# A three-sublayer decoder kernel on one core: new orders at four places of an iteration, x2's halves in exchanged banks, and the third residual's sums on GpSimd

## The reference, cut to what matters

```
x = layernorm(x + attention(x))         # q, k, v, 16 heads of 32, causal softmax, output projection, with biases
x = layernorm(x + wkv(decay, first, k=x, v=ctx))   # a recurrence over the 256 tokens, each channel alone
x = layernorm(x + gated_attention(x))   # 16 heads of q; ONE shared k and v per token: those of the head
                                        # whose gate is highest (v times the softmax value of that gate); causal
```

## Time and profile before

| what | value |
|---|---|
| median of 3 runs | 1510.12 us |
| the profiled execution's own time | 1509.66 us |
| its span, first to last instruction | 1507.8 us |
| mean granted TensorE clock | 0.989 |
| PE, DVE, ACT, POOL busy | 1397.5, 1095.7, 650.5, 378.6 us |

### The profile page before, as it was taken

One profiled execution on the slowest core, in us unless ns is written; L12 is line 12 of the kernel. 1 busy time (PEld: TensorE's weight loads), 2 busy tenths in 40 slices (PEclk: granted clock), 3 DMA queues, 4 the chain that ended last, 5 costly groups with the idle time before them and its releaser, 6 DMA issues.

```text
span 1507.8 us, 26652 instructions
## 1 busy us (share of the span) xinstructions
PE 1397.5 (93%) x9908; PEld 1112.9 (74%) x9908; DVE 1095.7 (73%) x2258; ACT 650.5 (43%) x1459; POOL 378.6 (25%) x520
## 2 busy tenths in 40 slices
PE   7887899999999999999999999999999999998796
PEld 6676778777777877777777777777777777876563
DVE  4464777777777777777777778777787776779753
ACT  3453435345353534535354453525444352544223
POOL 1244312222131222213122221312232232222200
PEclk9999999999999999999999999999999999999997
DMA  6531323324142332314333241333313233330210
GB/s 184 154 92 36 92 78 82 96 56 103 35 104 81 83 95 54 103 37 99 85 82 96 52 101 41 92 92 82 96 40 98 56 92 92 82 82 18 55 44 29
DMA packets 63199, 119.50 MB, mean 79 GB/s; under 512 B 14304, under 2 KB 32736, under 8 KB 63072
## 3 DMA queue, kind: packets, MB, share of 16 engines
q1 hardware_dynamic: 60128, 112.03, 29.4%
q10 hardware_dynamic: 2944, 5.77, 1.1%
HBM read 32.81 MB, written 8.39 MB: 27 GB/s over the span
## 4 chain that ended last, share of the span: by engine, by line
PE 63%; DVE 19%; issue 3%; SPq 2%; ACT 2%; DMA 1%; POOL 0%; ACTq 0%; POOLq 0%; DVEq 0%
PE po L591 7%; PE pp L486 6%; PE pp L488 6%; PE pp L487 6%; DVE neg_max L1527 5%; PE pw L486 4%; PE pw L488 4%; PE pw L487 4%; PE sk L564 3%; PE sq L532 3%; PE sk L511 3%; PE po L595 3%; PE po L605 3%; PE sq L511 3%; PE sq L526 2%
## 5 line engine op out<-in xcount | busy, mean ns | idle before, releaser
L1527 DVE TENSOR_REDUCE neg_max<-sq 128x2 f32<-128x512 f32 (+1 forms) x384 | 252.7, 686 | 126.7 <-PE sq L511 125.1
L1161 ACT ACTIVATE prob<-sk 128x512 f32<-128x512 f32 x384 | 215.9, 597 | 250.7 <-PE sk L511 248.0
L486 PE MATMUL pp<-xt_hi,w_hi 128*128 128x256 f32 x616 | 189.1, 307 | 18.7 <-DVE w_lo L1514 7.6
L488 PE MATMUL pp<-xt_hi,w_lo 128*128 128x256 f32 x616 | 175.8, 285 | 0.0
L487 PE MATMUL pp<-xt_lo,w_hi 128*128 128x256 f32 x616 | 175.7, 285 | 0.0
L1172 ACT ACTIVATE o_ch<-po 128x512 f32<-128x512 f32 x128 | 76.2, 595 | 167.0 <-PE po L595 167.0
L486 PEld LDWEIGHTS pp<-xt_hi,w_hi 128*128 128x128 f32 x616 | 120.0, 195 | 23.2 <-issue 19.4
L2048 POOL TENSOR_TENSOR w_ev<-w_e,w_val 128x256 f32<-128x256 f32 x64 | 45.8, 716 | 360.0 <-ACT w_e L1218 319.3
L511 PE MATMUL sk<-mask_kq,ident_b 128*128 128x256 bf16 (+1 forms) x384 | 124.4, 324 | 0.0
L511 PE MATMUL sq<-mask_qk,ident_b 128*128 128x256 bf16 (+1 forms) x384 | 124.4, 324 | 0.0
L487 PEld LDWEIGHTS pp<-xt_lo,w_hi 128*128 128x128 f32 x616 | 119.6, 194 | 0.3
(11 more groups left out here) (203 smaller groups left out, 3679.6 us busy)
## 6 DMA issues: line engine op xcount, KB each, us to landing
q_stack<-q_hi SPq DMA_DIRECT2D x256, 128.0 KB, 2.4
q_stack<-q_lo SPq DMA_DIRECT2D x128, 128.0 KB, 2.4
k_stack<-k_hi SPq DMA_DIRECT2D x128, 128.0 KB, 2.3
x_raw<-in_xT SPq DMA_DIRECT2D x16, 512.0 KB, 3.9
k_stack<-k_lo SPq DMA_DIRECT2D x64, 128.0 KB, 2.3
x<-in_x SPq DMA_DIRECT2D x16, 512.0 KB, 4.4
w_val<-in_ctxT SPq DMA_DIRECT2D x64, 128.0 KB, 2.2
out_y<-x SPq DMA_DIRECT2D x13, 512.0 KB, 2.8
```

The source lines that it names most:

```text
L486: T.matmul(out, lh, rh, start=(c == 0), stop=False, skip_group_check=True)
L488: mm = T.matmul(out, ll, rh, start=False, stop=(c == CC - 1), skip_group_check=True)
L1161: A.activation(dst, sk[n % 2][:], ACT.Exp, scale=SCALE).then_inc(s_exp, 1)
L1527: V.tensor_reduce(dst, src, AX.X, ALU.max, negate=True).then_inc(s_max, 1)
```

## The change

Four edits of order, one of banks, and one that moves an operation between engines.

1. `x2_transpose` puts half 0 into `pp` and half 1 into `pw`, in this order; the splits read the exchanged banks. `project_f(b, PF_Q)` waits at its first matmul for `pf_free` only (half 0), and for `u_free` (half 1) before channel chunk 2 of 4.
2. VectorE: `out_lo(t, 0)` goes ahead of `divide(r, 2)`.
3. ScalarE: `out_hi(t, 1)` goes ahead of `exps_a(t, 2, 2)`.
4. VectorE: `maxima_f(b, 1, 0, 1)` goes ahead of `pick_value(b, 1)`.
5. For b = 0 to 12 the additions of the third residual are made by GpSimd (`third_sum`), each announced by `f_added`. `normalise` waits until the sum before it has read `o_tok`; `third_stats` waits for all four sums. For b = 13 and 14, and for the last sequence, VectorE adds as before.

```diff
+F_LINKS_SENT = F_LINKS - 4
...
+        def added_by_pool(b):
+            return b < LAST - 2
...
             def x2_transpose(b):
                 pe.wait_ge(x2_ready, b + 1)
+                pe.wait_ge(pa_free, values_done(min(b + 2, NB)))
+                wait(pe, pf_free, PF_JOBS * b)
+                turn_half(pp, x_of(b), 0).then_inc(pf_job, 1)
...
-                turn_half(pw, x_of(b), 0).then_inc(u_job, 1)
-
-                pe.wait_ge(pa_free, values_done(min(b + 2, NB)))
-                wait(pe, pf_free, PF_JOBS * b)
-                turn_half(pp, x_of(b), 1).then_inc(pf_job, 1)
+                turn_half(pw, x_of(b), 1).then_inc(u_job, 1)
...
             def project_f(b, job, middle=None):
+                each = None
                 if job == PF_Q:
-                    pe.wait_ge(u_free, U_JOBS * b + U_X2 + 1)
+                    def each(c):
+                        if c == HC:
+                            pe.wait_ge(u_free, U_JOBS * b + U_X2 + 1)
...
-                    mm = channels_out(bank, W_FQ, job - PF_Q, middle)
+                    mm = channels_out(bank, W_FQ, job - PF_Q, middle, each=each)
...
                 exps_a(t, 2, 0, 1)
+                out_hi(t, 1)
                 exps_a(t, 2, 2)
-                out_hi(t, 1)
...
-            def normalise(ch, b, g, s_po, s_norm):
+            def normalise(ch, b, g, s_po, s_norm, added=0):
                 dve.wait_ge(s_po, NG * b + g + 1)
+                wait(dve, f_added, added)
...
-                normalise(ch, b, g, a_po, a_norm)
+                normalise(ch, b, g, a_po, a_norm, NG * (b - 2))
...
-                normalise(ch, b, g, f_po, f_norm)
+                normalise(ch, b, g, f_po, f_norm, NG * b + g if added_by_pool(b) else 0)
+                if added_by_pool(b):
+                    return
                 dve.wait_ge(f_norm, NG * b + g + 1)
                 cols = slice(P * g, P * (g + 1))
                 ch.link(V.tensor_tensor(x[:, :, cols], x[:, :, cols], o_tok[:], ALU.add))
...
             def third_stats(b, x):
+                if added_by_pool(b):
+                    dve.wait_ge(f_added, NG * (b + 1))
                 ln_stats(ch, 2, x)
...
                 sums(r, 3)
+                out_lo(t, 0)
                 divide(r, 2)
-                out_lo(t, 0)
...
                     rows_f(b, 0)
+                    maxima_f(b, 1, 0, 1)
                     pick_value(chf, b, 1)
-                    maxima_f(b, 1, 0, 1)
...
+            def third_sum(b, g):
+                if b < 0 or not added_by_pool(b):
+                    return
+                x = x_of(b)
+                pool.wait_ge(f_norm, NG * b + g + 1)
+                cols = slice(P * g, P * (g + 1))
+                G.tensor_tensor(x[:, :, cols], x[:, :, cols], o_tok[:], ALU.add).then_inc(f_added, 1)
...
             def iteration(t, last=False):        # GpSimd's
                 r, b = t - 1, t - 2
+                third_sum(b - 1, NG - 1)
                 weighted(r, 2)
...
                 if last:
                     return
+                third_sum(b, 0)
                 weighted(t, 0)
+                third_sum(b, 1)
                 weighted(t, 1)
                 products(t, 0)
+                third_sum(b, 2)
                 products(t, 1)
                 quotient(t, 0)
                 quotient(t, 1)
```

More of the change, by code:

```diff
@@ L197, in build @@
         a_pv, a_och, f_pv, f_och = sem("a_pv"), sem("a_och"), sem("f_pv"), sem("f_och")
-        a_po, a_norm, f_po, f_norm = sem("a_po"), sem("a_norm"), sem("f_po"), sem("f_norm")
+        a_po, a_norm, f_po, f_norm, f_added = sem("a_po"), sem("a_norm"), sem("f_po"), sem("f_norm"), sem("f_added")
         a_stk = [sem(f"a_stk{g}") for g in range(NG)]
@@ L292, in chain_f @@
             s_f, at = links_f(b)
-            ch = Chain(V, s_f, F_LINKS, at)
-            ch.n = n
+            ch = Chain(V, s_f, F_LINKS_SENT if added_by_pool(b) else F_LINKS, 0)
+            ch.base, ch.n = F_LINKS_SENT * at, n
             return ch
@@ L298, in wait_links_f @@
             s_f, at = links_f(b)
-            eng.wait_ge(s_f, F_LINKS * at + n)
+            eng.wait_ge(s_f, F_LINKS_SENT * at + n)
         def values_done(b):
@@ L1357, in x2_split_hi @@
             def x2_split_hi(b):
-                for half, s_job, count, bank in ((0, u_job, U_JOBS * b + U_X2 + 1, pw),
-                                                 (1, pf_job, PF_JOBS * b + PF_X2 + 1, pp)):
+                for half, s_job, count, bank in ((0, pf_job, PF_JOBS * b + PF_X2 + 1, pp),
+                                                 (1, u_job, U_JOBS * b + U_X2 + 1, pw)):
                     act.wait_ge(s_job, count)
@@ L1622, in x2_split_lo @@
                 part = slice(HC * half, HC * (half + 1))
-                bank, s_free = ((pw, u_free), (pp, pf_free))[half]
+                bank, s_free = ((pp, pf_free), (pw, u_free))[half]
                 V.tensor_tensor(xt_lo[:, part, :].rearrange("p c t -> p (c t)"), bank[:],
@@ L1718, in last_third_residual @@
                 ch = chain_f(b)
-                ch.n = F_LINKS - 3
+                ch.n = F_LINKS_SENT - 2 if added_by_pool(b) else F_LINKS - 3
                 third_residual(ch, b, NG - 1, x)
@@ L1723, in third_stats @@
                 ch = chain_f(b)
-                ch.n = F_LINKS - 1
+                ch.n = ch.per - 1
+                if added_by_pool(b):
+                    dve.wait_ge(f_added, NG * (b + 1))
                 ln_stats(ch, 2, x)
```

## The result

The changed kernel takes 1461.68 us, the median of four runs (1458.87 to 1463.56). The kernel before took 1509.69 in as many beside it. The ratio is 0.9677, with a 95% interval of 0.9656 to 0.9698: 3.2% faster. The forecast was 1459.5. The profiled execution took 1463.56 us with a span of 1461.8.

The account below looks back on a forecast made before the run. TensorE's nearly closed stream was taken as the bound, its pauses ended by VectorE's order. Iterations 2 to 15 give 14 x 3.50 = 49.0, iteration 1 2.0, the last sequence 0.7, less 1.4: 50.3 us off, 1459.5 us; range 1452 to 1485.

Parts of the forecast that it names:

- rivals 2 and 5: Rival 2: only B goes, 1486 (0.14 together with Rival 3); rival 5: the change does nothing, 1510 us (0.03).
- A: TensorE's stall before the first projection of x2, waiting for both halves: 0.41 + 0.15, 0.56 us an iteration saved.
- B: TensorE's stall before max_a(t, 2), with out_lo(t, 0) behind the reciprocal: 1.38 + 0.15 = 1.53 us an iteration saved.
- C: TensorE's stall before max_a(t, 3), with out_hi(t, 1) behind the third exponential: 0.29 + 0.15 = 0.44 us an iteration saved.
- D: TensorE's stall before sq_f(b, 1, 2), with the maxima behind pick_value(b, 1): 0.82 + 0.15 = 0.97 us an iteration saved.
- 0.15 us a place: Added at each of A to D, since in a closed stream matmuls overlap: 0.6 us an iteration over the bracketed 2.90.
- The sums on GpSimd: Third residual's sums: VectorE gives up 1.84 us an iteration, counted as nothing; third_stats 0.47 us later, no loss.
- the cover of sk_a(t, 1): Time left before sk_a(t, 1) needs the row maxima's DMA: 1.8 us, less 0.47, less 0.56, leaves 0.8.
- Rival 1: Late third_stats or maxima's DMA at sk_a(t, 1) or sk_a(t, 2): new waits of 0.4 to 1.3 us, 1471 us; chance 0.2.
- Rival 3: Each of four GpSimd sums blocks VectorE for 0.49 us, 25 us given back, 1484; chance 0.14 together with rival 2.
- Rival 4: Hand-over at third_stats makes TensorE stand every iteration; gain used up at 5.2 us, 1520 at 6 us; chance 0.05.
- Iteration 1: Stands 2.31 us at B; out_lo saves 1.6, and about 0.4 for C: 2.0 us saved.

Follow-up runs that it names:

- no_c: The changed kernel with edit 3 taken back, ScalarE's third exponential of group 2 ahead of out_hi(t, 1) again: 1470.77 us, ratio 0.9736.
- the doses: The changed kernel with one, two or three idle GpSimd operations ahead of the sum of group 3: 1468.02, 1479.54 and 1504.80 us.
- dose_3: The changed kernel with three idle GpSimd operations ahead of the sum of group 3: 1504.80 us, ratio 0.9949.
- rows_first: The changed kernel with two idle GpSimd operations ahead of the sum of group 3 and VectorE's rows_a(t, 1) ahead of third_stats: 1473.64 us, ratio 0.9745.
- no_b: The changed kernel with edit 2 taken back, the reciprocal of divide(r, 2) ahead of out_lo(t, 0) again: 1481.59 us, ratio 0.9812.
- dose_2: The changed kernel with two idle GpSimd operations ahead of the sum of group 3: 1479.54 us, ratio 0.9792.

## Why the prediction was right

**The reading of the bound** held, and with it rivals 2 and 5 fell: each of A to D has its own price, and no wait on VectorE took the place of one. TensorE's pauses were the only time to be had, and A to D gave all of it: the iteration is 3.60 us shorter (3.58 from split to split), forecast 3.50 less 0.1. Adding 0.15 us a place to the bracketed idle time was right on the whole: 2.90 were in brackets, 3.51 came by starts. A gave 0.65 (forecast 0.56), B 1.44 (1.53), C 0.45 (0.44), D 0.97 (0.97).

**A.** Right. Chunks 0 and 1 cover the second half's "lo". The exchange of banks costs and gives nothing by itself.

**B.** Right. 0.1 us to spare was forecast, 0.28 is seen.

**C.** Right. Its price by ratio without the edit, 8.9 us, is higher than the 6.6 that the steps give (14 x 0.44 + 0.4). The trace of no_c accounts for 7; the rest lies within the intervals of the two ratios.

**D.** Right, and the pick that was put behind the maxima hurts nobody: the next projection into its bank does not wait.

**The sums on GpSimd** were counted at nothing, and two experiments, with and without the other edits, find nothing. The duration, 0.73 us, is the one forecast. So is the hand-over, nearly: third_stats start 0.84 us after the normalisation's end (679.84 + 0.42 to 681.10), forecast 0.93. With VectorE's own sum it was 0.50 (699.88 + 0.42 to 700.80), so they are 0.34 us later, forecast 0.47. **The step that was mis-sized is the cover of sk_a(t, 1)**: 0.8 us were worked out and the doses show 0.3. The transfer's bytes were seen 1.8 us ahead of the matmul, and "for the semaphore" I left what remained. From the end of rows_a to the matmul it takes 1.84 us (in dose_3: 792.62 + 0.25 to 794.71). With it the changed trace has 685.12 - 682.84 - 1.84 = 0.44 as the upper bound of the cover, near the 0.3 of the doses. In the trace of before rows_a ended at 702.53 (702.28 + 0.25), so sk_a(t, 1) could have started at 704.37, 0.4 us behind the last bytes at 704.0: this 0.4 is the error. A second mistake beside it: the way over VectorE's queue to max_a(t, 2) was not named as a way for the late sum, and rows_first shows that it is as short: of 1.6 us, less the 0.25 of rows_a, 1.1 arrive. Neither mistake touched the time, since 0.3 us of cover were still left behind the sum's own delay and A's gain.

**Rival 1, a thin cover tears**, did not come at the places that it named: in iterations 2 to 15 of the changed trace neither sk_a(t, 1) nor sk_a(t, 2) waits for its DMA. But the prediction's own sign of being wrong, waits of line 569 (now 573) on the row DMA, is there in small, before sk_a(t, 0): 7 from 165 us on, where there had been 4.

**Rival 3, the two engines blocking each other**, did not come. The scans of w_e (now line 1603) last 867 ns on the mean, as before at 866, and the statistics 683 as before. The pair that blocked in the trace before was VectorE's own third sum against a product of GpSimd's, in 13 of its 64 sums. The edit takes this sum out of VectorE's queue, and GpSimd's next product lasts 0.74 us instead of 0.91. The rule of the Trainium skill (SBUF — State Buffer, "Who interferes with whom") is not contradicted, and not tested: no operation of VectorE with two tensors of SBUF runs beside a new sum. Those of groups 0 to 2 meet maxima and a "lo" subtraction, which read PSUM, a reciprocal, and the normalising of x (line 1577), which lasts 0.59 us in all 13 cases and at most 0.55 elsewhere.

**Rival 4, slower by the hand-over**, was the right mechanism for a wrong kernel: dose_3 is what it would take. Its threshold was put at 5.2 us of sum and hand-overs; with the measured cover it is 0.84 + 0.3 + 3.6 = 4.7 (an estimate). With three operations more they take 0.84 + 2.43 = 3.3 us and some 8 us of the gain are left by ratio. The clock was not in the rival's price, and it is a third of dose_3's.

**The total.** The medians are 48.0 us apart, the forecast had 50.3; part of the nearness is luck, since errors of both signs stand in it. From the first to the last split of x2 (ScalarE, 167.8 to 1423.0 before, 168.4 to 1378.0 after) the kernel is 45.6 us shorter. The iterations give 14 x 3.60 = 50.4, where 14 x 3.40 had been forecast. Two things take from it:

- The two DMA entries grew by 2.3 us in 6 more waits; with 0.15 us a wait that is 3.2 (an estimate). The forecast had set 1.4 aside for thin covers and had not named these two places. Why they come mainly in the last iterations stays open.
- The stretch before the last split takes 45.13 us (1332.82 to 1377.95) in place of 43.77 (1379.19 to 1422.96). Its 214 matmuls keep TensorE busy for 34.76 us in place of 32.89, at a mean clock of 0.95 in place of 1.00, although x2's second half no longer holds TensorE for 0.86 us there.

Iteration 1 was forecast with 2.0 us and is 2.9 shorter (from the matmul shown below to the first split: 95.93 us before, 93.08 after), but the trace does not bear the forecast's sum out. Its wait at B fell from 2.31 to 0.63 us and the one at C, 1.00 us, is gone; DMA waits of 0.85 and 1.05 us stand there now, where one of 0.34 had been, and TensorE's idle time fell by 1.0 us in all. The other 1.9 us are busy time of the same 568 matmuls: before, the clock was 0.83 over the 10 us behind the wait at B, and now it stays at 1.00.

In the profiled execution the opening, which the change does not touch, was 3.5 us longer. TensorE's first matmul of iteration 1's projections in the trace before, and after:

```profile
71.85 0.36 PE L486 MATMUL pp<-xt_hi,w_hi 128*128 128x256 f32 x1 [0.88 <-DVE x L1662]
```
```profile
75.33 0.36 PE L490 MATMUL pp<-xt_hi,w_hi 128*128 128x256 f32 x1 [0.88 <-DVE x L1670]
```

Ahead of it TensorE waited 2.17 us for a row DMA at 39.09 (0.63 us before), and the clock was low behind this wait, as it was for a shorter time in the stretch before the last split, behind a wait of 3.26 us. By stretch:

```profile
39.00:50.00 11.00, 10.33 (x49) 7.68 (x50) 2.33 (x4) 3.11 (x7) 0.00 (x0) 0.53 0.40 90
1355.00:1361.00 6.00, 4.47 (x15) 3.65 (x16) 3.69 (x7) 0.00 (x0) 1.11 (x2) 0.72 0.09 19
```

The first split of x2 stands at 166.2 in no_c's trace and at 169.1 in no_b's, so the opening scatters by some us from one execution to the next.

## What to carry to other kernels

Where one engine's stream is nearly closed, list its few pauses and ask of each which instruction of the releasing engine stood needlessly ahead: three swaps of neighbours and one split wait, with the exchange of banks that it needs, gave 3.2% here, and taking them back one by one shows that their prices add. Moving work off an engine that is 73% busy gave nothing, because it released none of those pauses sooner. A hand-over to another engine right ahead of a queue's critical instructions needs its cover measured, from the end of the delayed instruction to the start of the one that waits; here bytes seen on a queue came 0.4 us before the waiter could have started. And where two kernels' times are close, the length of one undisturbed iteration in their traces settles what the medians cannot.

## What the runs showed of the hardware that was not expected

A pause of TensorE can cost more than its length. In dose_3, behind a wait of 1.81 us, the mean granted clock was 0.83 in place of 1.00 over the next 10 us (1.00 is 2.4 GHz; 0.83 is a mean of time there and time at 1.2 GHz), and the iteration was 1.6 us longer; behind a wait of 1.82 us in another iteration it was 1.00. It fell behind 10 of the 13 such waits. What sets them apart was not found. The waits of 1.01 us (dose_2) and 1.38 us (the kernel before) left it at 1.00. The length does not decide alone: at the same place near the end a wait of 3.15 us in the kernel before left it at 1.00 and one of 3.26 us in the changed kernel did not, and in iteration 1 of rows_first it was 0.85 over the 10 us behind a wait of 1.08 us. And a stream with 84.27 us busy of 84.50 kept the full clock.
